# Softmax denominators in causal attention: the adds of the diagonal tiles moved from TensorE to GpSimd

## The chip, the cores and the metric

One core of a Trainium2 chip runs the whole kernel in one launch. The metric is the device time in microseconds of one execution; lower is better. The times of the kernel before are three executions.

## The reference, cut to what matters

The kernel computes one decoder layer for x of shape (2, 2048, 512): causal self-attention with 16 heads of 32 columns, cross-attention over 77 context rows, and a mixture of 8 experts, each followed by a layer norm. The change lies in the self-attention:

```python
dots = jnp.einsum('bhid,bhjd->bhij', q, k) * scale
causal_mask = jnp.triu(jnp.ones((t, t), dtype=bool), 1)
dots = jnp.where(causal_mask, -jnp.inf, dots)
attn = jax.nn.softmax(dots, axis=-1)
out = jnp.einsum('bhij,bhjd->bhid', attn, v)
```

The softmax of a query divides by the sum of its exponentials over all keys up to its own position. That sum, the denominator, is what the change computes in another way.

## The kernel before, in words

The kernel has three phases: the projections (`project`), the self-attention (`self_attention`), and everything else (`second_half`). The phases follow each other; each ends with a barrier of all engines.

**Tiles.** The self-attention goes through 8 groups (2 batches of 4 groups), each with 4 heads. In a group the 2048 queries are cut into 4 chunks of 512 (c = 0 to 3), and the keys into tiles of 128 (kt). Chunk c needs the tiles kt = 0 to 4c + 3. The last four of them lie on the diagonal: there only the queries from `off` = 0, 128, 256 or 384 on see the keys, so these tiles are 512, 384, 256 and 128 columns wide. The others are called whole. A chunk has 4, 8, 12 or 16 tiles, a group 40, and each tile has four units, one for each head: 160 units in a group.

**Steps.** All engines run the same list of steps, one step for each unit, two groups to a turn of the hardware loop (`laps`). What an engine does in a step is fixed by a lag: the function `chunk_at(s, lag)` names the chunk whose last unit lay `lag` steps ago, `tile_at(s, lag)` the tile. Each engine takes its work strictly in this order. Counted from the last unit of a chunk (step 0), and for tile j of the chunk that follows (its units are steps 4j + 1 to 4j + 4):

- step of the unit itself: TensorE makes the scores of keys by queries in `st_ps` (a ring of 3, L821 and L824), ScalarE takes the exponentials into `probs` (a ring of 5 tiles, L715).
- `VALUES` = 4: TensorE multiplies the tile with the values into `o_ps` (L841), four heads side by side, fp32.
- `SUMS` = 6: TensorE multiplies the tile with ones into `den_ps` (L859): the denominator. This is done for the diagonal tiles and for every third whole tile.
- lag 1: GpSimd adds the other whole tiles (kt % 3 is not 2) into `total` (L623). The tiles 0, 1, 3, 4, 6 and so on are taken; the first add reads tiles 0 and 1 and so comes with tile 1. Tile j is added in step 4j + 5. After the last sum of a chunk TensorE multiplies `total` with ones (L864) and closes the denominator.
- steps 5 and 7: ScalarE moves `o_ps` to `o_raw` (L721) and `den_ps` to `den` (L725).
- `RECIPS` = 9, 11, 13, 15: VectorE takes the reciprocal of `den` in four pieces (L767).
- `SCALED` = 16: GpSimd multiplies `o_raw` by `den` into `o_sb` (L629).
- step 18: VectorE makes the fp16 high part of `o_sb` (L772, a copy with a cast). Step 19: GpSimd subtracts it for the low part (L633). Step 20: SyncE stores both.

**The row maxima.** Beside this, and ahead of it, TensorE makes the same scores as queries by keys in `s_ps` (a ring of 3, L804 and L807) and VectorE reduces each to its row maxima (L746). When a chunk's maxima are complete, three small VectorE instructions make `max_parts` of them (L750, L752, L755), TensorE turns these to rows (L793), VectorE moves the rows out (L742) and SyncE copies them into `q_pair`, where the score matmuls of the chunk take them in. This side work (`AUX`) is spread over the steps by a planner (`schedule`) that weighs VectorE's costs. By its plan the rows of chunk 3 are turned in the second unit of the third diagonal tile of chunk 2, those of chunk 2 at unit 10 of chunk 1 (9 after the change), those of the next group's chunk 0 at unit 10 of chunk 3 (9 after), and those of its chunk 1 in the middle of chunk 3. Counted here from 1.

**Order.** TensorE's step is: scores, one piece of side work, values, sums, the rest of the side work. VectorE's step is: side work, reciprocals, cast. GpSimd's step is: add, multiply, subtract.

Of the kernel before, what the change touches and what calls it, by code (L numbers as in the profile page):

```python
# [6 lines left out]
ALU, ACT, AX = mybir.AluOpType, mybir.ActivationFunctionType, mybir.AxisListType  # L7
# [6 lines left out]
P = 128  # L14
# [5 lines left out]
CPB = T // CH  # L20
TT = CH // P
# [380 lines left out]
def self_attention(nc, S, x_rows, q_parts, k_parts, v_rows, o_parts):  # L402
# [17 lines left out]
    for c in range(CPB):  # L420
# [1 line left out]
    NKU, NVU, NAUX = len(KU), len(VU), len(AUX)  # L422


    POOLED = [[n for n, (k, kt) in enumerate(KU) if k == c and kt < c * TT and kt % 3 != 2]
              for c in range(CPB)]
    ADDS = [n for tiles in POOLED for n in tiles[1:]]
    NP = 5
# [1 line left out]
    PIECES = 4  # L430

    VALUES, SUMS = 4, 6
    TAKEN = VALUES + 1, SUMS + 1
    RECIPS = [SUMS + 3 + 2 * n for n in range(PIECES)]
    SCALED = RECIPS[-1] + 1
    STORED = SCALED + 4
    TAIL = STORED + 1
# [96 lines left out]
    with ExitStack() as stack:  # L534
# [31 lines left out]
        st_ready = Count(nc, stack, "st_ready", 2 * NVU)  # L566
        exp_done = Count(nc, stack, "exp_done", 2 * NVU)
        pv_done = Count(nc, stack, "pv_done", 2 * NKU)
        o_ready = Count(nc, stack, "o_ready", 2 * CPB)
        o_taken = Count(nc, stack, "o_taken", 2 * CPB)  # L570
        den_taken = Count(nc, stack, "den_taken", 2 * CPB)
        added = Count(nc, stack, "added", 2 * len(ADDS))
# [11 lines left out]
        def _(pool):  # L584
# [25 lines left out]
            def step(i, s, first, end):  # L610
                k = tile_at(s, 1, first, end)
                if k is not None and k % NKU in ADDS:
                    c, n = KU[k % NKU][0], adds_upto(k) - 1
                    starts = k % NKU == POOLED[c][1]
                    pool.wait_ge(exp_done.sem, exp_done.at(i, HG * k + HG - 1))
                    if starts:

                        pool.wait_ge(pv_done.sem, pv_done.at(i, k // NKU * NKU + LAST_TILE[c - 1]))
                        other = probs[:, (k // NKU * NKU + POOLED[c][0]) % NP]
                    else:  # L620
                        pool.wait_ge(added.sem, added.at(i, n - 1))
                        other = total[:]
                    nc.gpsimd.tensor_tensor(total[:], other, probs[:, k % NP], ALU.add).then_inc(added.sem, 1)  # L623
                c = chunk_at(s, SCALED, first, end)
                if c is not None:

                    pool.wait_ge(recips.sem, recips.at(i, c * PIECES + PIECES - 1))
                    pool.wait_ge(split_done.sem, split_done.at(i, c - 1))
                    nc.gpsimd.tensor_tensor(o_sb[:], o_raw[:], den[:], ALU.mult).then_inc(scaled.sem, 1)  # L629
                c = chunk_at(s, SCALED + 3, first, end)  # L630
                if c is not None:
                    pool.wait_ge(o_hi_done.sem, o_hi_done.at(i, c))
                    nc.gpsimd.tensor_tensor(o_out[:, c % 2, 1], o_sb[:], o_out[:, c % 2, 0],  # L633
                                            ALU.subtract).then_inc(split_done.sem, 1)
# [64 lines left out]
        def _(act):  # L699
# [4 lines left out]
            def step(i, s, first, end):  # L704
# [11 lines left out]
                                         scale=SCALE).then_inc(exp_done.sem, 1)  # L716
                c = chunk_at(s, TAKEN[0], first, end)
                if c is not None:
                    act.wait_ge(o_ready.sem, o_ready.at(i, c))
                    act.wait_ge(scaled.sem, scaled.at(i, c - 1))  # L720
                    nc.scalar.activation(o_raw[:], o_ps[:], ACT.Copy).then_inc(o_taken.sem, 1)  # L721
                c = chunk_at(s, TAKEN[1], first, end)
                if c is not None:
                    act.wait_ge(pv_done.sem, pv_done.at(i, c // CPB * NKU + LAST_TILE[c % CPB]))
                    nc.scalar.activation(den[:], den_ps[:], ACT.Copy, scale=1.0 / XS).then_inc(den_taken.sem, 1)  # L725

            laps(act, step)
# [49 lines left out]

        @block.tensor
        def _(pe):
            for count in (st_ready, pv_done, o_ready, s_ready):  # L780
                count.lead(pe)

            def aux(i, n):
# [45 lines left out]
            def values(i, k):  # L829
# [12 lines left out]
                                            start=(kt == 0), stop=final)  # L842
                if k % NKU in POOLED[c]:
                    last.then_inc(pv_done.sem, 1)
                elif final:
                    last.then_inc(o_ready.sem, 1)

            def sums(i, k):

                c, kt = KU[k % NKU]  # L850
                off, pooled = max(kt - c * TT, 0) * P, POOLED[c]
                final = k % NKU == LAST_TILE[c]
                if k % NKU in pooled:
                    return
                opens = all(n in pooled for n, (x, _) in enumerate(KU) if x == c and n < k % NKU)
                if opens:
                    pe.wait_ge(den_taken.sem, den_taken.at(i, k // NKU * CPB + c - 1))
                for h, out in enumerate(heads):
                    last = nc.tensor.matmul(den_ps[out, off:], ones[:], probs[:, k % NP, h, off:], start=opens,  # L859
                                            stop=final and not pooled)  # L860
                if final and pooled:
                    pe.wait_ge(added.sem, added.at(i, adds_upto(k) - 1))
                    for h, out in enumerate(heads):
                        last = nc.tensor.matmul(den_ps[out, :], ones[:], total[:, h], start=False, stop=True)  # L864
                last.then_inc(pv_done.sem, 1)

            def step(i, s, first, end):
                p = unit_at(s, 0, first, end)
# [8 lines left out]
                k = tile_at(s, SUMS, first, end)  # L877
                if k is not None:
                    sums(i, k)
                for n in todo[1:]:  # L880
                    aux(i, n)

# [672 lines left out]
```

## Time and profile before

| | us |
|---|---|
| three executions | 2785.82, 2792.28, 2791.89 |
| median | 2791.89 |
| the profiled execution, its own time | 2788.14 |
| its span, first to last instruction | 2786.3 |
| TensorE busy (92% of the span) | 2563.3 |
| VectorE busy (69%) | 1913.3 |
| ScalarE busy (40%) | 1102.4 |
| GpSimd busy (28%) | 782.0 |

The self-attention lies between about 325 and 1517 us. Engines in the rows: PE is TensorE (matmuls), PEld its weight loads, DVE VectorE, ACT ScalarE, POOL GpSimd, SP SyncE. A row of a timeline has the start, the duration, the engine, the line and operation, output and inputs, the shapes, and the number of instructions merged into it; in brackets stands how long the engine was idle before it and what ended that. One fp32 matmul of L841, L859 or L864 is recorded as two, so one tile with its four heads is 8 records.

### The profile page before, as it was taken

Reading aid. Unit: us, or ns where it says so; the run is one execution under the profiler, and the core shown is the slowest. Engines: PE = TensorE matmul, PEld = TensorE weight load, DVE = VectorE, ACT = ScalarE, POOL = GpSimd, SP = SyncE. Lnnn points to the kernel's source line nnn. Section 1 sums busy time; section 2 is a strip of 40 time slices with the busy share of each in tenths; the row PEclk is TensorE's granted clock in tenths of the full one; section 3 lists DMA queues with packets and bytes.
Section 4 is the critical chain, followed back from the end, with each engine's and each line's share of the span. In section 5 each row is a group of like instructions: output and inputs, shape, how many; then the busy total and the mean of one; then the engine's idle time right before and its main releaser. Section 6 shows DMA issues by size and latency. Waiting matters only on the chain. (4 is left out here: it accounts for less than half of the span.)

```text
span 2786.3 us, 44691 instructions
## 1 busy us (share of the span) xinstructions
PE 2563.3 (92%) x15124; PEld 1064.3 (38%) x15124; DVE 1913.3 (69%) x3125; ACT 1102.4 (40%) x2002; POOL 782.0 (28%) x276
## 2 busy tenths in 40 slices
PE   8999699998999899999998679999999999999998
PEld 3444223232232233332322335454544544454543
DVE  5442787877778677778882557776867676767764
ACT  4231155555555455555555223231323323232320
POOL 0000254553636344445455211111201011111100
PEclk9999799999999999999999889999999999999999
DMA  7953500302020302012001210101010101001000
GB/s 245 306 193 140 122 9 6 73 6 70 9 69 9 69 6 55 23 34 74 5 12 56 86 43 1 58 1 59 1 43 16 43 16 43 16 1 58 1 16 16
DMA packets 115902, 146.74 MB, mean 53 GB/s; under 512 B 9086, under 2 KB 87678, under 8 KB 114653
## 3 DMA queue, kind: packets, MB, share of 16 engines
q1 hardware_dynamic: 115677, 143.77, 16.9%
q8 instruction: 138, 2.26, 0.3%
q14 instruction: 87, 0.71, 0.1%
HBM read 91.57 MB, written 51.91 MB: 51 GB/s over the span
## 5 line engine op out<-in xcount | busy, mean ns | idle before, releaser
L715 ACT ACTIVATE probs<-st_ps 128x512 f32<-128x512 f32 (+3 forms) x1280 | 628.2, 533 | 590.5 <-PE st_ps L821 294.6
L746 DVE TENSOR_REDUCE seg_max<-s_ps 128x1 f32<-128x512 f32 (+3 forms) x1280 | 699.8, 599 | 230.3 <-PE s_ps L804 136.9
L804 PE MATMUL s_ps<-k_pair,q_pair 96*128 96x512 f16 (+3 forms) x1280 | 438.7, 364 | 70.0 <-DVE seg_max L746 56.4
L821 PE MATMUL st_ps<-q_pair,k_pair 98*128 98x512 f16 (+3 forms) x1280 | 434.6, 360 | 26.6 <-issue 19.5
L623 POOL TENSOR_TENSOR total<-total,probs 128x2048 f32<-128x2048 f32 x88 | 398.2, 4525 | 62.1 <-ACT probs L715 59.6
L841 PE MATMUL o_ps<-probs,v_sb 128*32 128x512 f32 (+3 forms) x2560 | 321.4, 572 | 0.7 <-issue 0.7
L1381 PE MATMUL fps<-x2T,w_p_hi 128*128 128x512 f16 x1024 | 317.2, 379 | 0.0
L1381 PE MATMUL fps<-w_p_hi,hT 128*128 128x512 f16 x1024 | 306.0, 381 | 0.0
L821 PEld LDWEIGHTS st_ps<-q_pair,k_pair 98*128 98x128 f16 x1280 | 117.5, 98 | 374.4 <-ACT probs L715 287.4
L804 PEld LDWEIGHTS s_ps<-k_pair,q_pair 96*128 96x128 f16 x1280 | 125.6, 99 | 276.9 <-DVE seg_max L746 191.3
L1343 DVE SCALAR_TENSOR_TENSOR x<-fps,gates_un,x 128x512 f32<-128x512 f32 x256 | 184.0, 746 | 36.0 <-PE fps L1381 33.4
L623 POOL TENSOR_TENSOR total<-probs 128x2048 f32<-128x2048 f32 x24 | 108.8, 4533 | 354.7 <-ACT probs L715 354.7
L1168 ACT ACTIVATE hidden<-fps,keep_b_sb 128x512 f32<-128x512 f32 x128 | 86.5, 687 | 304.1 <-PE fps L1381 303.8
L1381 PE MATMUL fps<-w_p_lo,hT 128*128 128x512 f16 x512 | 194.7, 380 | 0.0
L1381 PE MATMUL fps<-x2T,w_p_lo 128*128 128x512 f16 x512 | 194.0, 379 | 0.0
L1085 POOL TENSOR_TENSOR rstd<-rstd,keep_power 128x4 f32<-128x4 f32 x24 | 26.2, 1090 | 552.0 <-DVE rstd L1206 552.0
L1100 POOL TENSOR_TENSOR soft<-soft,ssum 128x1232 f32<-128x1232 f32 x32 | 72.9, 2288 | 384.4 <-DVE ssum L1236 384.4
L1332 DVE TENSOR_SCALAR hT<-hidden 128x512 f16<-128x512 f32 x128 | 86.0, 672 | 108.1 <-ACT hidden L1168 107.5
L859 PE MATMUL den_ps<-probs,ones 128*32 128x512 f32 (+3 forms) x1472 | 156.0, 494 | 0.0
L1381 PEld LDWEIGHTS fps<-x2T,w_p_hi 128*128 128x128 f16 x1024 | 100.2, 98 | 128.8 <-issue 5.9
L1381 PEld LDWEIGHTS fps<-w_p_hi,hT 128*128 128x128 f16 x1024 | 98.1, 98 | 131.0 <-issue 20.8
L767 DVE RECIPROCAL den<-den 128x128 f32<-128x128 f32 x128 | 116.5, 927 | 44.5 <-ACT den L725 44.5
(162 smaller groups left out, 3553.7 us busy)
## 6 DMA issues: line engine op xcount, KB each, us to landing
k_pair<-k_parts SPq DMA_DIRECT2D x96, 128.0 KB, 5.0
q_pair<-q_parts SPq DMA_DIRECT2D x96, 128.0 KB, 5.6
x_raw<-xT_in SPq DMA_DIRECT2D x8, 1024.0 KB, 6.5
q_parts<-qk_out SPq DMA_DIRECT2D x32, 256.0 KB, 3.6
k_parts<-qk_out SPq DMA_DIRECT2D x32, 256.0 KB, 4.0
piece_raw<-w_in SPq DMA_DIRECT2D x8, 1024.0 KB, 8.7
v_rows<-v_out SPq DMA_DIRECT2D x32, 256.0 KB, 2.1
w_parts<-piece_cut SPq DMA_DIRECT2D x8, 1024.0 KB, 5.6
```

What stands on the lines that cost most here:

```text
L623: nc.gpsimd.tensor_tensor(total[:], other, probs[:, k % NP], ALU.add).then_inc(added.sem, 1)
L715: nc.scalar.activation(probs[:, k % NP, h, off:], st_ps[:, p % (2 * NVU) % RING, off:], ACT.Exp, scale=SCALE).then_inc(exp_done.sem, 1)
L746: nc.vector.reduce_max(seg_max[:, h, j, s:s + 1], s_ps[:, slot, 0:width], AX.X).then_inc(s_read.sem, 1)
L767: nc.vector.reciprocal(piece, piece).then_inc(recips.sem, 1)
L804: last = nc.tensor.matmul(s_ps[:, slot, 0:width], q_pair[a][0:NR, h, q0:q0 + P], k_pair[a][0:NR, h, s * CH:s * CH + width], start=True, st ...
L821: last = nc.tensor.matmul(st_ps[:, slot, off:], k_pair[a][:, h, kt * P:(kt + 1) * P], q_pair[a][:, h, c * CH + off:(c + 1) * CH], start=Tr ...
L841: last = nc.tensor.matmul(o_ps[out, off:], v_sb[a][:, kt, out], probs[:, k % NP, h, off:], start=(kt == 0), stop=final)
L859: last = nc.tensor.matmul(den_ps[out, off:], ones[:], probs[:, k % NP, h, off:], start=opens, stop=final and not pooled)
L1168: nc.scalar.activation(hidden[:, n % 2], fps[:, (u * NUNIT + f) % FB], ACT.Gelu, bias=W["b1_sb"][:, n:n + 1], scale=UN).then_inc(gelu_done ...
L1332: nc.vector.tensor_scalar(hT[:, 0, e % 2, j], hidden[:, n % 2], XS, None, ALU.mult).then_inc(h_hi.sem, 1)
L1343: nc.vector.scalar_tensor_tensor(x2[q][:, j], bank, gates_un[q][:, j, e:e + 1], x2[q][:, j], ALU.mult, ALU.add).then_inc(added.sem, 1)
L1381: last = nc.tensor.matmul(bank, lhs(a, t), rhs(b, t), start=(n == 0), stop=(n == len(steps) - 1))
```

## The change

GpSimd's list of tiles takes in the diagonal tiles as well. Its first add of chunk 0 is 384 columns wide and followed by a copy of the 128 columns that only tile 0 has. TensorE's sums are left for every third whole tile only; `total` is multiplied with ones in a step of its own, `TOTALS` = 8, for all four chunks (before: chunks 1 to 3, in step 6). The steps that hang on it follow two later: `den` is moved in step 9, the reciprocals are in steps 11, 13, 15 and 17, the multiply in step 18, the cast in step 20, the subtraction in step 21, the store in step 22. The first add of a chunk waits for the totals of the chunk before. SyncE's loads for the group after next wait for `pv_done` of a group's last tile, which now comes with its values.

```diff
-    POOLED = [[n for n, (k, kt) in enumerate(KU) if k == c and kt < c * TT and kt % 3 != 2]
+    POOLED = [[n for n, (k, kt) in enumerate(KU) if k == c and (kt >= c * TT or kt % 3 != 2)]
               for c in range(CPB)]
...
     VALUES, SUMS = 4, 6
-    TAKEN = VALUES + 1, SUMS + 1
-    RECIPS = [SUMS + 3 + 2 * n for n in range(PIECES)]
+    TOTALS = 8
+    TAKEN = VALUES + 1, TOTALS + 1
+    RECIPS = [TOTALS + 3 + 2 * n for n in range(PIECES)]
     SCALED = RECIPS[-1] + 1
...
                     pool.wait_ge(exp_done.sem, exp_done.at(i, HG * k + HG - 1))
+                    off = max(KU[k % NKU][1] - c * TT, 0) * P
                     if starts:
-                        pool.wait_ge(pv_done.sem, pv_done.at(i, k // NKU * NKU + LAST_TILE[c - 1]))
+                        pool.wait_ge(den_ready.sem, den_ready.at(i, k // NKU * CPB + c - 1))
                         other = probs[:, (k // NKU * NKU + POOLED[c][0]) % NP]
                     else:
                         pool.wait_ge(added.sem, added.at(i, n - 1))
                         other = total[:]
-                    nc.gpsimd.tensor_tensor(total[:], other, probs[:, k % NP], ALU.add).then_inc(added.sem, 1)
+                    last = nc.gpsimd.tensor_tensor(total[:, :, off:], other[:, :, off:], probs[:, k % NP, :, off:],
+                                                   ALU.add)
+                    if starts and off:
+                        last = nc.gpsimd.tensor_copy(total[:, :, 0:off], other[:, :, 0:off])
+                    last.then_inc(added.sem, 1)
...
-                    act.wait_ge(o_ready.sem, o_ready.at(i, c))
+                    act.wait_ge(pv_done.sem, pv_done.at(i, c // CPB * NKU + LAST_TILE[c % CPB]))
                     act.wait_ge(scaled.sem, scaled.at(i, c - 1))
...
-                    act.wait_ge(pv_done.sem, pv_done.at(i, c // CPB * NKU + LAST_TILE[c % CPB]))
+                    act.wait_ge(den_ready.sem, den_ready.at(i, c))
...
             def sums(i, k):
                 c, kt = KU[k % NKU]
-                off, pooled = max(kt - c * TT, 0) * P, POOLED[c]
-                final = k % NKU == LAST_TILE[c]
-                if k % NKU in pooled:
+                if k % NKU in POOLED[c]:
                     return
...
                 for h, out in enumerate(heads):
-                    last = nc.tensor.matmul(den_ps[out, off:], ones[:], probs[:, k % NP, h, off:], start=opens,
-                                            stop=final and not pooled)
-                if final and pooled:
-                    pe.wait_ge(added.sem, added.at(i, adds_upto(k) - 1))
-                    for h, out in enumerate(heads):
-                        last = nc.tensor.matmul(den_ps[out, :], ones[:], total[:, h], start=False, stop=True)
+                    last = nc.tensor.matmul(den_ps[out, :], ones[:], probs[:, k % NP, h], start=opens, stop=False)
                 last.then_inc(pv_done.sem, 1)
+
+            def totals(i, c):
+                opens = all(n in POOLED[c % CPB] for n, (x, _) in enumerate(KU) if x == c % CPB)
+                if opens:
+                    pe.wait_ge(den_taken.sem, den_taken.at(i, c - 1))
+                pe.wait_ge(added.sem, added.at(i, adds_upto(c // CPB * NKU + LAST_TILE[c % CPB]) - 1))
+                for h, out in enumerate(heads):
+                    last = nc.tensor.matmul(den_ps[out, :], ones[:], total[:, h], start=opens, stop=True)
+                last.then_inc(den_ready.sem, 1)
...
                 k = tile_at(s, SUMS, first, end)
                 if k is not None:
                     sums(i, k)
+                c = chunk_at(s, TOTALS, first, end)
+                if c is not None:
+                    totals(i, c)
```

## Rows read from the trace of the kernel before

**Rows 1.** The page, part 1: busy time and share of the span

```profile
PE 2563.3 (92%) x15124; PEld 1064.3 (38%) x15124; DVE 1913.3 (69%) x3125; ACT 1102.4 (40%) x2002; POOL 782.0 (28%) x276
```

**Rows 2.** Stretches: busy us of each engine, granted clock share (PEclk), DMA share, GB/s

```profile
340.00:1517.00 1177.00, 1086.01 (x7734) 350.29 (x7734) 900.26 (x1483) 645.29 (x1327) 582.65 (x176) 0.96 0.13 32
```

**Rows 3.** Groups by shape, 440 to 1520 us: busy us, mean ns of one record

```profile
L859 PE MATMUL den_ps<-probs,ones 128*32 128x512 f32 x648 | 86.7, 604 | 0.0
...
L859 PE MATMUL den_ps<-probs,ones 128*32 128x384 f32 x232 | 24.7, 498 | 0.0
...
L864 PE MATMUL den_ps<-total,ones 128*32 128x512 f32 x176 | 22.9, 592 | 0.0
...
L859 PE MATMUL den_ps<-probs,ones 128*32 128x256 f32 x232 | 18.5, 391 | 0.0
...
L859 PE MATMUL den_ps<-probs,ones 128*32 128x128 f32 x232 | 12.8, 294 | 0.0
```

**Rows 4.** TensorE's timeline: one denominator sum and the matmul behind it

```profile
622.82 1.06 PE L859 MATMUL den_ps<-probs,ones 128*32 128x512 f32 x8
...
623.82 0.28 PE L821 MATMUL st_ps<-q_pair,k_pair 98*128 98x256 f16 x1
```

**Rows 5.** Single lines: duration ns min/median/max, first and last start us

```profile
L772 DVE CAST o_out<-o_sb x32: 415/3682/4746, 358.9 to 1515.5; 128x512 f16<-128x512 f32 x32
...
L752 DVE TENSOR_SCALAR max_parts<-row_max x32: 174/175/1448, 294.5 to 1461.0; 128x16 f16<-128x16 f32 x32
...
L755 DVE SCALAR_TENSOR_TENSOR max_parts<-row_max,max_parts x32: 174/174/176, 295.5 to 1461.3; 128x16 f16<-128x16 f32 x32
```

**Rows 6.** Timelines of POOL, DVE, ACT and PE, start of chunk 2 of a group

```profile
692.12 1.27 POOL L629 TENSOR_TENSOR o_sb<-o_raw,den 128x512 f32<-128x512 f32 x1 [1.71 <-DVE den L767]
693.36 4.52 POOL L623 TENSOR_TENSOR total<-total,probs 128x2048 f32<-128x2048 f32 x1
...
694.94 3.22 DVE L772 CAST o_out<-o_sb 128x512 f16<-128x512 f32 x1
...
689.74 2.07 ACT L715 ACTIVATE probs<-st_ps 128x512 f32<-128x512 f32 x4 [1.20 <-PE st_ps L821]
...
694.55 1.09 ACT L715 ACTIVATE probs<-st_ps 128x512 f32<-128x512 f32 x2 [1.10 <-PE st_ps L821]
...
698.69 0.39 PE L804 MATMUL s_ps<-k_pair,q_pair 96*128 96x512 f16 x1 [1.98 <-DVE seg_max L746]
```

**Rows 7.** Stretches behind two stalls, and the longer stall in TensorE's timeline

```profile
699.90:703.70 3.80, 3.59 (x12) 0.57 (x12) 2.78 (x5) 1.22 (x3) 3.80 (x1) 0.55 0.19 69
...
649.80:655.80 6.00, 5.99 (x28) 1.35 (x29) 2.19 (x5) 2.87 (x6) 1.94 (x1) 0.50 1.00 226
...
649.81 0.61 PE L821 MATMUL st_ps<-q_pair,k_pair 98*128 98x512 f16 x1 [5.99 <-issue]
```

**Rows 8.** Timelines, start of chunk 3 of the last group, and its end

```profile
1472.01 4.54 POOL L623 TENSOR_TENSOR total<-probs 128x2048 f32<-128x2048 f32 x1 [12.13 <-ACT probs L715]
...
1477.73 4.55 POOL L623 TENSOR_TENSOR total<-total,probs 128x2048 f32<-128x2048 f32 x1
...
1477.82 4.75 DVE L772 CAST o_out<-o_sb 128x512 f16<-128x512 f32 x1 [2.96 <-POOL o_sb L629]
...
1510.15 0.60 ACT L725 ACTIVATE den<-den_ps 128x512 f32<-128x512 f32 x1 [0.48 <-PE den_ps L864]
```

**Rows 9.** Timelines of ACT, DVE and PE, diagonal tiles of chunk 2

```profile
555.02 2.20 ACT L715 ACTIVATE probs<-st_ps 128x512 f32<-128x512 f32 x4 [1.15 <-PE st_ps L824]
...
559.98 0.17 DVE L752 TENSOR_SCALAR max_parts<-row_max 128x16 f16<-128x16 f32 x1
...
560.68 0.33 PE L793 MATMUL s_ps<-ident,max_parts 128*8 128x128 f16 x3
```

**Rows 10.** TensorE's timeline in chunk 0: its unit 7, and unit 5 of chunk 1

```profile
486.50 0.34 PE L821 MATMUL st_ps<-q_pair,k_pair 98*128 98x384 f16 x1
...
495.95 0.39 PE L821 MATMUL st_ps<-q_pair,k_pair 98*128 98x512 f16 x1
```

More of the change, by code:

```diff
@@ L568, in self_attention @@
         pv_done = Count(nc, stack, "pv_done", 2 * NKU)
-        o_ready = Count(nc, stack, "o_ready", 2 * CPB)
+        den_ready = Count(nc, stack, "den_ready", 2 * CPB)
         o_taken = Count(nc, stack, "o_taken", 2 * CPB)
@@ L779, in _ @@
         def _(pe):
-            for count in (st_ready, pv_done, o_ready, s_ready):
+            for count in (st_ready, pv_done, den_ready, s_ready):
                 count.lead(pe)
@@ L844, in values @@
                     last.then_inc(pv_done.sem, 1)
-                elif final:
-                    last.then_inc(o_ready.sem, 1)
             def sums(i, k):
                 c, kt = KU[k % NKU]
-                off, pooled = max(kt - c * TT, 0) * P, POOLED[c]
-                final = k % NKU == LAST_TILE[c]
-                if k % NKU in pooled:
+                if k % NKU in POOLED[c]:
                     return
-                opens = all(n in pooled for n, (x, _) in enumerate(KU) if x == c and n < k % NKU)
+                opens = all(n in POOLED[c] for n, (x, _) in enumerate(KU) if x == c and n < k % NKU)
                 if opens:
```

## The prediction

> **What bounds the kernel now.** I read the busy shares first: TensorE works 92% of the span [rows 1]. The row for the attention alone says 1086 of 1177 us for TensorE, 900 for VectorE and 583 for GpSimd [rows 2]. So TensorE sets the pace, a matmul taken away there is worth its slot, and GpSimd has room on average. Then I asked where TensorE's missing 91 us go. The timeline around a chunk's start answers it [rows 6]: VectorE's cast L772 takes 3.22 us, while its shortest takes 0.415 us and its median 3.68 us [rows 5]. It lies over a GpSimd add of 4.52 us and ends just after it. TensorE runs out of free `s_ps` slots and stands still for 1.98 us. This happens once in each of chunks 1, 2 and 3 (24 times; I found stalls of 1.7 to 2.7 us). So the copying cast cannot run while GpSimd adds. The order of GpSimd's queue is therefore part of TensorE's path, and this is what the change moves.
>
> After such a stall TensorE's clock falls. Behind the 1.98 us stall the granted clock is 0.55 for 3.8 us, practically 1.2 GHz in place of 2.4, which costs about 1.8 us. Behind the stall of 5.99 us at the loop's turn it is 0.50 for 6.0 us, which costs 3.0 us [rows 7].
>
> **The change, part by part.** The sum is made against the profiled execution's own time, 2788.1 us, which is 0.13% under the median of the three runs.
>
> *Sums removed on TensorE.* The groups by shape give 1.07, 0.85, 0.64 and 0.44 us busy for a tile of 512, 384, 256 and 128 columns (86.7 us for 648 records, 8 to a tile; 24.7, 18.5 and 12.8 us for 232) [rows 3]. The next matmul starts 1.00 us after the start of a 512 sum that is 1.06 long [rows 4], so a slot is 0.07 shorter or so: 1.00 + 0.78 + 0.57 + 0.36 = 2.7 us for each of 32 chunks, 86.7 us. Chunk 0 gets a total that it did not have, 8 x 1.0 us. The totals of the other chunks only move. Net: **-78 us**. I take all of it, as TensorE is the pace there. If exponentials (ScalarE) were late in the short tiles, perhaps 10 us of it would be lost.
>
> *GpSimd's load.* An operation on 512 elements takes 1.27 us, one on 2048 takes 4.52 [rows 6], so by a line through both 1024 take 2.4 and 1536 take 3.4. The four diagonal adds are 11.6 us, those of chunk 0 with its copy about 7.7 (the copy of 512 elements is not in the trace; between 0.2 and 1.27 us, I take 0.6, half of the nearest row, as it reads one operand). That is 42.5 us a group, 340 in all, and raises GpSimd to 923 of 1177 us. It does not become the bound on average, and its total is there in time: the diagonal adds end some 4 to 5 us after a chunk's last exponential, and TensorE asks for them 8 steps later, 6 us or more.
>
> *The chunk start, chunks 1 to 3.* Before, GpSimd's queue was: multiply (step 16), add of tile 3 (17), while the cast stood in step 18. Now it is: add of tile 3 (17), multiply (18), add of tile 4 (21), with the cast in step 20. The multiply waits behind one add, and the cast behind the multiply and then behind the next add. In the chunk shown: the exponentials of tile 3 end at 689.74 + 2.07 = 691.8, so the add of tile 3 runs from 691.9 to 696.4 and the multiply to 697.7. The exponentials of tile 4 ended at 695.6, so its add follows at once, to 702.2. The cast ends at 702.6, one reduction frees a slot, and TensorE goes on at 703.2 instead of 698.7 [rows 6]. It stands two steps further on by then. Between the exponentials at 689.74 and 694.55 lie six steps, so two are 1.6 us, and the loss is 4.5 - 1.6 = 2.9 us more than before. Does the add really get in ahead of the waiting cast? At the start of the last group's chunk 3 VectorE had waited 2.96 us for the multiply, the add began 0.1 us before the cast, and the cast took 4.75 us, the longest of all [rows 8]. So yes. 23 starts (that last one has no reductions left to hold up): **+67 us**. The lower end is a gain (the third rival), the upper 3.2 us each, 74. The stalls grow to about 5 us, between the two of rows 7; I take 2.4 us for the slow clock behind each in place of 1.8: **+14 us**.
>
> The Trainium skill has the rule in "SBUF — State Buffer", section "SBUF: two separate sides": VectorE and GpSimd share a port pair that is an exclusive lock for the whole instruction, taken by whichever starts first. By that rule the trace agrees with its 4.75 us cast, and the sum stays the same.
>
> *The rows of chunk 3.* `max_parts` are made while chunk 2's diagonal tiles are exponentiated. Before, no GpSimd add ran then. Now the add of tile 8 starts when its exponentials end, at 557.2, and runs to 561.8; L752 would start at 559.98, inside it [rows 9]. L752 can be held up: its median is 0.175 us, its longest 1.448 [rows 5]. At 561.8 the add of tile 9 is ready too and takes 3.4 us, to 565.3. If it gets in first, as in rows 8, L752 and L755 end at about 565.7 instead of 560.35. TensorE needs them at 560.68 and has nothing to pass the time with, since the turn L793 stands in its queue: 5.0 us x 8 = **+40 us**, and 2.4 us of slow clock x 8 = **+19 us**. If VectorE gets in first with both, it is 1.8 us a group. L755 itself was never slowed (176 ns at most [rows 5]).
>
> The same section of the Trainium skill says that VectorE operations with two SBUF inputs, which L755 is, need the pair as well; then the add of tile 9 would come between L752 and L755 if not before both, and the whole 5 us would be paid either way. No row here shows it.
>
> *Chunk 0.* The cast of chunk 3 comes in step 20, when chunk 1 of the next group has begun, and ScalarE's `o_raw` in step 21 waits for the same multiply. GpSimd's chain from the total on is 3.4 + 0.6 + 2.4 + 1.3 + 1.3, with gaps some 9.5 us. TensorE has from unit 7 to unit 5 of chunk 1 9.45 us [rows 10], less two units and a values step (2.0) and three sums (2.35), plus four more units, values and total that it can still do (3.6): 8.7 us. So it waits about 1 us, in 5 of the 7 boundaries (**+5 us**; at the other two it stands at the loop's turn anyway). Bounds: 0 and 3 us each. The group loads on SyncE start some 2 us earlier; nothing waited for them but the loop's turn, whose 6 us I leave as they are.
>
> *The end.* Chunk 3 of the last group has no side work and GpSimd is its pace. From its first add at 1472.01 to ScalarE's `den` at 1510.15 it took 38.1 us [rows 8]. Now the chain is 7 adds of 4.52, the multiply and subtraction (2.5), the cast (0.4), the diagonal adds (11.6) and the total (1.0): 47.2 us, so 9 us more, and the 2.7 us of sums counted above are not won: **+12 us**.
>
> Sum: -78 + 67 + 14 + 40 + 19 + 5 + 12 = +79, so **2867 us**.
>
> **The rivals.** *A, the forecast*, 2867 us; its own range is 2845 to 2892 from the ends named above. Chance 0.45.
>
> *B, VectorE gets in at the end of the add of tile 8.* Then the rows cost 1.8 us and about 1 us of clock a group, 22 in place of 59: 2830 us. For it: L752 has been waiting for 2 us by then, while the cast of rows 8 had only just been released. Chance 0.22.
>
> *C, more of the small instructions are caught.* Chunk 2's `max_parts` fall half a microsecond before the first add of chunk 1 starts; if that add gets them, up to 4.5 us x 8 come on top, or the slow clock lasts longer than I took: about 2900 us. Chance 0.15.
>
> *D, faster.* The cast gets in between the multiply and the add of tile 4. The point that decides is that instant, 24 times. The cast would end at 698.1 where VectorE reaches it at 696.5, no TensorE stall remains, and the old ones go too (24 x 2.1 us and 24 x 1.8 us of clock): -78 - 51 - 43 + 14 + 5 + 12 = -141, 2647 us. A mixture of both outcomes would lie just under the old time. Against it stands the 4.75 us cast. Chance 0.13.
>
> *E, the terms cancel.* The stalls grow by 1 us only, because the reductions left in the ring carry TensorE further, and the rows as in B: -78 + 23 + 22 + 17 = -16, up to +10 with the clock. Chance 0.05.
>
> **How the numbers follow.** A and C end over, B too. The range goes from half way between B and E, 2805, to C's upper part, 2905; it leaves D, E and the far end out. A measurement here tells 0.3%, 8 us, from no change. Faster: D and part of E, 0.14. The same: 0.05. Slower: 0.81.
>
> **What would show it.** Right: the median of L772 at 5 to 7 us or, where the wait for the multiply is counted apart, casts near 4.7 behind idle time; TensorE stalls of 4 to 5 us at the starts of chunks 1 to 3; L752 or L755 at 2 to 5 us once a group, and as much idle before L793; GpSimd busy near 1120 us of the span; TensorE's L859 down to 448 records, L864 up to 256. Wrong: casts of 0.4 us behind the multiply, or TensorE stalls as short as before. Waits of L864 for the adds would be a further rival that I give no weight.

## The result and the profile after

The changed kernel takes 2874.06 us (median of 4 runs, 2871.89 to 2876.44) against 2790.48 us for the kernel before in the same comparison: a ratio of 1.0302, with an interval of 1.0284 to 1.032. It is slower, as forecast. The profiled execution took 2871.89 us against 2788.14 before, 83.8 us more. In the changed kernel the lines of the code stand 6 further down for VectorE, ScalarE and TensorE's score steps (the cast L772 is now L778, L752 and L755 are L758 and L761, the turn L793 is L799, the reductions L746 are L752), and 2 further down for GpSimd's add (L625); its multiply L629 is now L635, its copy L628. TensorE's values are L847, its sums L861 and its totals L871. ScalarE's exponentials are L721, `o_raw` is L727 and `den` L731.

The page of the kernel after, its busy times, the granted clock and GpSimd over 40 slices, and the group of the cast (columns as in [rows 1]):

```profile
PE 2512.6 (88%) x14164; PEld 1063.0 (37%) x14164; DVE 1960.2 (68%) x3125; ACT 1094.8 (38%) x2002; POOL 1119.7 (39%) x404
...
POOL 0001377776677767776778321020112111111100
PEclk9999889898898989898999779999999999999999
...
L778 DVE CAST o_out<-o_sb 128x512 f16<-128x512 f32 x32 | 115.2, 3600 | 67.1 <-POOL o_sb L635 67.1
```

GpSimd is busy for 1119.7 us, the 1120 of the prediction, and the 32 casts wait 67.1 us in all for the multiply L635 and then run for 3.6 us on average. The 24 at the starts of chunks 1 to 3 take 4.6 to 4.75 us each, the 8 others 0.43 us.

The attention's stretch of the kernel after, which is 84 us longer than in [rows 2] (same columns), and the stretch around the stall at a start of chunk 2:

```profile
340.00:1601.00 1261.00, 1034.48 (x6776) 347.55 (x6772) 942.00 (x1478) 636.01 (x1325) 913.00 (x300) 0.90 0.12 29
...
719.50:726.50 7.00, 7.00 (x22) 1.91 (x23) 4.57 (x9) 2.17 (x4) 0.56 (x1) 0.54 0.12 40
```

TensorE's work in the attention fell from 1086.0 to 1034.5 us, so 51.5 us were won. But its idle time rose from 91.0 to 226.5 us, by 135.5. The difference is the 84 us that the kernel lost. The waits of TensorE over the whole execution say who ended that idle time (us in all, how often, the longest), first in the kernel before, then after:

```profile
PE s_ps L804 <- DVE seg_max L746: 56.4, 49, 2.7
...
PE s_ps L793 <- DVE max_parts L755: 13.2, 9, 2.8
```

```profile
PE s_ps L810 <- DVE seg_max L752: 137.5, 55, 5.8
PE s_ps L799 <- DVE max_parts L761: 39.1, 17, 3.1
PE o_ps L847 <- ACT o_raw L727: 12.8, 5, 3.0
```

The third had no counterpart before. Taken one by one, the 23 stalls at the starts of chunks 1 to 3 rose from 50.8 to 130.5 us. All but one (5.09 us) are now 5.6 to 5.8 us long, where they were 1.7 to 2.7. The timeline of the kernel after around the same start of chunk 2 as in [rows 6] shows why (start, duration, engine, line, operation, and in brackets the idle time before it and its releaser):

```profile
708.32 4.54 POOL L625 TENSOR_TENSOR total<-total,probs 128x2048 f32<-128x2048 f32 x1 [1.18 <-ACT probs L721]
...
712.83 1.27 POOL L635 TENSOR_TENSOR o_sb<-o_raw,den 128x512 f32<-128x512 f32 x1
...
714.05 4.50 POOL L625 TENSOR_TENSOR total<-total,probs 128x2048 f32<-128x2048 f32 x1
...
714.13 4.70 DVE L778 CAST o_out<-o_sb 128x512 f16<-128x512 f32 x1 [2.06 <-POOL o_sb L635]
...
719.49 0.61 PE L810 MATMUL s_ps<-k_pair,q_pair 96*128 96x512 f16 x1 [5.76 <-DVE seg_max L752]
```

The multiply stands behind the add of tile 3. When it ends, the add of tile 4 is already queued and starts at once, 0.08 us ahead of the cast that the end of the multiply released. The cast then takes 4.70 us, where its shortest takes 0.43, and ends 0.28 us behind the add. VectorE's reductions stand behind it, TensorE gets no free slot of `s_ps`, and stands still for 5.76 us.

The diagonal of chunk 2 in the kernel after, which answers to [rows 9]:

```profile
572.58 4.51 POOL L625 TENSOR_TENSOR total<-total,probs 128x2048 f32<-128x2048 f32 x1
...
577.17 3.46 POOL L625 TENSOR_TENSOR total<-total,probs 128x1536 f32<-128x1536 f32 x1
...
573.60 3.53 DVE L758 TENSOR_SCALAR max_parts<-row_max 128x16 f16<-128x16 f32 x1
577.16 0.18 DVE L761 SCALAR_TENSOR_TENSOR max_parts<-row_max,max_parts 128x16 f16<-128x16 f32 x1
577.39 0.28 PE L799 MATMUL s_ps<-ident,max_parts 128*8 128x128 f16 x2 [3.03 <-DVE max_parts L761]
```

L758 can do nothing until the add of tile 8 ends (572.58 plus 4.51 is 577.09) and is done at 577.13. L761 starts at 577.16, 0.01 us ahead of the add of tile 9. That is one stall of 3.0 to 3.1 us in each of the 8 groups.

The last group's chunk 3 in the kernel after, from GpSimd's first add to ScalarE's `den` (same columns):

```profile
1544.70 4.54 POOL L625 TENSOR_TENSOR total<-probs 128x2048 f32<-128x2048 f32 x1 [2.77 <-PE den_ps L871]
...
1591.94 1.93 PE L871 MATMUL den_ps<-total,ones 128*32 128x512 f32 x8 [10.62 <-POOL total L625]
1593.94 0.60 ACT L731 ACTIVATE den<-den_ps 128x512 f32<-128x512 f32 x1 [11.95 <-PE den_ps L871]
```

It takes 49.2 us, against 38.1 in [rows 8]. TensorE's wait of 10.62 us for the last add is part of it.

### The profile page after: what moved, and what is told of

It reads as the page before. It is cut to its first block and busy times, and to the rows that moved or that the text cites. A ratio compares the mean times of both kernels' runs of the same rounds, so it can differ in the third digit from the quotient of the medians.

```text
span 2870.1 us, 43117 instructions
## 1 busy us (share of the span) xinstructions
PE 2512.6 (88%) x14164; PEld 1063.0 (37%) x14164; DVE 1960.2 (68%) x3125; ACT 1094.8 (38%) x2002; POOL 1119.7 (39%) x404
## 5 line engine op out<-in xcount | busy, mean ns | idle before, releaser
L721 ACT ACTIVATE probs<-st_ps 128x512 f32<-128x512 f32 (+3 forms) x1280 | 619.9, 536 | 654.3 <-PE st_ps L827 336.3
L752 DVE TENSOR_REDUCE seg_max<-s_ps 128x1 f32<-128x512 f32 (+3 forms) x1280 | 697.8, 598 | 177.1 <-PE s_ps L810 91.0
L625 POOL TENSOR_TENSOR total<-total,probs 128x2048 f32<-128x2048 f32 (+3 forms) x200 | 704.8, 3524 | 190.2 <-ACT probs L721 180.3
L810 PE MATMUL s_ps<-k_pair,q_pair 96*128 96x512 f16 (+3 forms) x1280 | 448.8, 375 | 153.7 <-DVE seg_max L752 137.5
L847 PE MATMUL o_ps<-probs,v_sb 128*32 128x512 f32 (+3 forms) x2560 | 328.3, 587 | 12.9 <-ACT o_raw L727 12.8
L625 POOL TENSOR_TENSOR total<-probs 128x2048 f32<-128x2048 f32 (+1 forms) x32 | 136.3, 4259 | 176.2 <-PE den_ps L871 138.1
L778 DVE CAST o_out<-o_sb 128x512 f16<-128x512 f32 x32 | 115.2, 3600 | 67.1 <-POOL o_sb L635 67.1
```

Source lines behind the costliest of these rows:

```text
L625: last = nc.gpsimd.tensor_tensor(total[:, :, off:], other[:, :, off:], probs[:, k % NP, :, off:], ALU.add)
L721: nc.scalar.activation(probs[:, k % NP, h, off:], st_ps[:, p % (2 * NVU) % RING, off:], ACT.Exp, scale=SCALE).then_inc(exp_done.sem, 1)
L752: nc.vector.reduce_max(seg_max[:, h, j, s:s + 1], s_ps[:, slot, 0:width], AX.X).then_inc(s_read.sem, 1)
L778: nc.vector.tensor_copy(o_out[:, c % 2, 0], o_sb[:]).then_inc(o_hi_done.sem, 1)
L810: last = nc.tensor.matmul(s_ps[:, slot, 0:width], q_pair[a][0:NR, h, q0:q0 + P], k_pair[a][0:NR, h, s * CH:s * CH + width], start=True, st ...
L847: last = nc.tensor.matmul(o_ps[out, off:], v_sb[a][:, kt, out], probs[:, k % NP, h, off:], start=(kt == 0), stop=final)
```

## The experiments

The theory (Q): GpSimd's own work costs nothing. What costs is that VectorE's copying instructions (the cast, the first of `max_parts`) can't run under a GpSimd add, and that the longer queue puts the multiply and the cast among the adds. One rival (L) says that 340 us more of GpSimd's work slow VectorE or the `probs` ring as such. Another (W) says that the cast only comes late, because the multiply waits behind an add, and VectorE's queue stands behind it. The results, each against the kernel before in the same comparison:

| run | median us | kernel before | ratio, interval |
|---|---|---|---|
| e1 change, cast on ScalarE | 2736.6 | 2789.15 | 0.9812, 0.9784 to 0.984 |
| e2 before, cast on ScalarE | 2723.7 | 2789.15 | 0.9767, 0.9737 to 0.9798 |
| e3 change, cast 4 steps later | 2791.11 | 2789.15 | 1.0005, 0.999 to 1.002 |
| e4 change without tile 4 | 2769.92 | 2789.15 | 0.9938, 0.992 to 0.9957 |
| e5 before, 11 of 16 sums left out | 2736.03 | 2790.49 | 0.9807, 0.9792 to 0.9821 |
| e6 change without tile 8 of chunk 2 | 2880.48 | 2790.49 | 1.0326, 1.0309 to 1.0342 |
| e7 change, two `o_raw` | 2900.32 | 2790.49 | 1.0392, 1.0375 to 1.0409 |
| e8 e1, two `o_raw`, high half on ScalarE | 2714.48 | 2790.49 | 0.9729, 0.9713 to 0.9745 |
| e10 e8, low half elsewhere too | 2666.16 | 2788.28 | 0.9564, 0.9549 to 0.9579 |
| e11 before, with e10's edits | 2702.57 | 2788.28 | 0.97, 0.9683 to 0.9717 |

**e1 and e2: the cast goes to ScalarE.** In both kernels the cast leaves VectorE. In e2 the steps are two lower, as TOTALS is not there.

```
-    STORED = SCALED + 4
+    STORED = SCALED + 8          (e2: + 6)
 ScalarE:
+                c = chunk_at(s, SCALED + 6, first, end)      (e2: + 4)
+                if c is not None:
+                    act.wait_ge(scaled.sem, scaled.at(i, c))
+                    act.wait_ge(o_stored[c % 2], stored_at(CPB * i + c // 2))
+                    nc.scalar.activation(o_out[:, c % 2, 0], o_sb[:], ACT.Copy).then_inc(o_hi_done.sem, 1)
 VectorE:
-                    nc.vector.tensor_copy(o_out[:, c % 2, 0], o_sb[:]).then_inc(o_hi_done.sem, 1)
```

> The changed kernel with the fp16 cast of o_sb moved from VectorE (step 20) to ScalarE (step 24, the subtraction follows in step 25). Theory Q (GpSimd's queue and the pair that VectorE's cast needs): the TensorE stalls of 5.6 to 5.8 us at the starts of chunks 1 to 3 vanish, 23 x 5.7 = 131 us, and most of the slow clock behind them (24 times 6.8 us at half speed, up to 80 us): 2660 to 2700 us. Rival L (GpSimd's 338 us of added work are the cost, whoever casts): within 10 us of the changed kernel, 2860 to 2880 us. Rival W (the wait for the late multiply is the cost, not the add that runs over the cast): ScalarE now waits in its place and TensorE's stalls come from the exponentials, about 2 us each: some 2790 us.

> The kernel before with the same cast on ScalarE (step 20, subtraction in step 21). Theory Q: its 24 stalls of 1.7 to 2.7 us (51 us) and the 1.7 us of slow clock behind each (41 us) vanish: about 2700 us. Rival L says nothing of it; if the stalls were only where TensorE loses slack that it needs anyway, under 20 us are won: 2770 us or more.

The changed kernel falls by some 137 us, to 2736.6, and the stalls at the chunk starts are gone. L falls as the main cause, since GpSimd does all the work of the change here. The kernel before gains 65 us by the same edit, so these stalls cost it as well; 89 were expected. And e1 misses its expectation by 37 us and stays 13 us behind e2. The waits of TensorE in e1 say where that is:

```profile
PE s_ps L801 <- DVE max_parts L768: 55.4, 18, 4.0
PE o_ps L849 <- ACT o_raw L728: 17.6, 7, 3.0
...
PE den_ps L873 <- POOL total L625: 15.3, 9, 10.6
```

and in e2:

```profile
PE s_ps L795 <- DVE max_parts L762: 23.6, 10, 4.1
```

So with the long stalls gone, the small instructions of `max_parts` and the late `o_raw` (0 us in e2) take 49 us more in e1 than in e2, and the waits for the adds (0 us in e2) another 15. Those are 65 of the 78 us of removed sums. The mean granted clock is lower too, 0.951 in e1 against 0.963 in e2; what that alone costs was not measured.

**e3: the cast stays on VectorE, four steps later.**

```
-    STORED = SCALED + 4
+    STORED = SCALED + 8
-                c = chunk_at(s, SCALED + 2, first, end)
+                c = chunk_at(s, SCALED + 6, first, end)      (the cast, on VectorE)
```

> The changed kernel with the cast still on VectorE, but four steps later (24 in place of 20; subtraction in 25). Theory Q: VectorE meets the add of tile 4 near its end instead of before its start, waits about 2.5 us in place of 6.5, and TensorE's stalls shrink from 5.7 to 1 or 2 us: 23 x 4 = 92 us and half of the slow clock behind them, 40 us: 2720 to 2760 us. Rival L: unchanged, 2870 us.

The cast in e3, as a single line (shortest, median and longest in ns, first and last start):

```profile
L778 DVE CAST o_out<-o_sb x32: 419/2480/4748, 364.2 to 1512.2; 128x512 f16<-128x512 f32 x32
```

83 us come back. The wait for the multiply is gone, but the cast still falls under some add: its median is 2.48 us, and the 23 stalls take 51.0 us, about what they took in the kernel before. I had expected at least 31 us more. A shift in steps changes how much of an add the cast meets, not that it meets one. The edit takes away W's wait and shortens the time under the add at once, so the 83 us can't be given to W alone. But W can't be all of it, as e1 has the same slack and is 55 us faster.

**e4: tile 4 of chunks 1 to 3 stays with TensorE.** No add is then queued right behind the multiply.

```
-    POOLED = [[n for n, (k, kt) in enumerate(KU) if k == c and (kt >= c * TT or kt % 3 != 2)]
+    POOLED = [[n for n, (k, kt) in enumerate(KU) if k == c and (kt >= c * TT or kt % 3 != 2) and not (c and kt == 4)]
```

> The changed kernel with tile 4 of chunks 1 to 3 summed by TensorE (24 sums of 1.0 us more) and not added by GpSimd, so that no add is queued behind the multiply when the cast is due. It keeps the wait for the multiply (1.2 to 2.0 us) and takes away the add over the cast. Theory Q: casts of 0.4 us, TensorE stalls under 1 us at those places: 2870 + 24 - 120 - 70 = about 2700 us. Rival W (the wait counts): stalls of 2 us stay, 2790 us. Rival L: GpSimd loses 108 us of work of 338, so a third of the loss, 2845 us.

The cast in e4, as a single line:

```profile
L778 DVE CAST o_out<-o_sb x32: 426/427/429, 362.5 to 1494.8; 128x512 f16<-128x512 f32 x32
```

All 32 casts now take 0.43 us, and the casts wait as long for the multiply as in the changed kernel (67.2 us in all against 67.1): one tile apart, 4.70 us have become 0.43. This is the cleanest proof that the add behind the multiply is what holds the cast. But 22 stalls of 1.3 to 1.9 us (33 us) stay. That is W's part, the wait for the multiply behind the add of tile 3. The time, 2769.9, lies nearer to W's 2790 than to Q's 2700. So of the 5.7 us of a stall some 1.5 are W's, and some 4 are the add's.

**e5: the kernel before with 11 of its 16 diagonal sums left out.** TensorE's gain alone, with nothing given to GpSimd: the denominators lack those tiles.

```
-                if k % NKU in POOLED[c]:
+                if k % NKU in POOLED[c] or left_out(k):
+            def left_out(k):
+                c, kt = KU[k % NKU]
+                return kt >= c * TT and kt < c * TT + 3 and kt > 0
```

> The kernel before with 11 of the 16 sums of diagonal tiles of a group left out on TensorE and given to nobody: the denominators miss those tiles. It measures the change's first term alone, with nothing added on GpSimd. By the slots, 3 x (1.00 + 0.78 + 0.57) + (0.78 + 0.57) = 8.4 us a group, 67 us in all. Theory Q: all of it is won, 2720 to 2730 us. Rival N (TensorE is not the pace in the short tiles, the exponentials are): half of it or less, 2750 us or more.

Of the 67 us expected 54.5 came. TensorE's busy time in the attention fell from 1084.9 to 1025.4 us, by 59.5, and the stalls stayed at 51 us. The 7.5 us of busy time that are missing go with the clock: its mean granted share over the span is 0.957 in the kernel before and 0.951 here. At two levels that is an estimated 240 and 268 us at the lower one, so up to 14 us lost. Another 3.5 us are TensorE's waits for exponentials (6.4 us before, 9.9 here), a small part of what rival N had forecast. The price by slot was about right, and the clock takes roughly a tenth of the gain.

**e6: tile 8 of chunk 2 stays with TensorE.** The add which held the first of `max_parts` is gone, and the add of tile 9 (1536 elements) is the next.

```
-    POOLED = [[n for n, (k, kt) in enumerate(KU) if k == c and (kt >= c * TT or kt % 3 != 2)]
+    POOLED = [[n for n, (k, kt) in enumerate(KU) if k == c and (kt >= c * TT or kt % 3 != 2) and not (c == 2 and kt == 8)]
```

> The changed kernel with the first diagonal tile of chunk 2 (tile 8) summed by TensorE, so that no long add runs while the row maxima of chunk 3 are made. Costs 8 sums, 8 us. Theory Q: the 3.0 us wait of the turn of rows, 8 times, goes, and with it some 12 us of slow clock: 2874 - 24 - 12 + 8 = about 2845 us. It also shows whether the third small instruction (two SBUF inputs) is held by the next add, of 1536 elements, which starts just then: if it is, waits of 3 us stay and the time is 2880 us.

The timeline of e6 on VectorE and GpSimd at the rows of chunk 3:

```profile
572.90 0.17 DVE L758 TENSOR_SCALAR max_parts<-row_max 128x16 f16<-128x16 f32 x1
573.08 3.42 POOL L625 TENSOR_TENSOR total<-total,probs 128x1536 f32<-128x1536 f32 x1 [1.31 <-ACT probs L721]
573.11 3.41 DVE L761 SCALAR_TENSOR_TENSOR max_parts<-row_max,max_parts 128x16 f16<-128x16 f32 x1
```

Nothing is won: the first instruction runs in 0.17 us, the add starts, and now the second, which starts 0.03 us behind it, is held for 3.41 us (3.33 to 3.42 in each of the 8 groups). It reads two SBUF operands of 128x16. This is the sentence of the Trainium skill that the prediction could not show by a row ("SBUF — State Buffer", section "SBUF: two separate sides": VectorE operations with two SBUF inputs need the shared pair too, against a GpSimd operation that reads SBUF, as this add does). By that rule, e6 agrees with 3.41 us against 0.18.

**e7: two buffers for `o_raw`.** ScalarE no longer waits for the multiply before it empties `o_ps`.

```
-        o_raw = sb("o_raw", [P, CH], F32)
+        o_raw = sb("o_raw", [P, 2, CH], F32)
-                    act.wait_ge(scaled.sem, scaled.at(i, c - 1))
-                    nc.scalar.activation(o_raw[:], o_ps[:], ACT.Copy).then_inc(o_taken.sem, 1)
+                    act.wait_ge(scaled.sem, scaled.at(i, c - 2))
+                    nc.scalar.activation(o_raw[:, c % 2], o_ps[:], ACT.Copy).then_inc(o_taken.sem, 1)
...
+                    act.wait_ge(scaled.sem, scaled.at(i, c - 1))       (ahead of den)
```

> The changed kernel with two buffers for o_raw, so that ScalarE's step 21 does not wait for the multiply of the chunk before. Theory Q: TensorE's wait of 2.4 to 3.0 us in chunk 1's second tile (5 times, 12.8 us) goes with 8 us of slow clock, if nothing comes in its place: 2855 us. VectorE's cast waits 3.0 us for the same multiply, so a stall of 1 us may take its place: 2862 us.

A miss in sign. The 12.8 us of waits for `o_raw` are gone, and the kernel is 26 us slower. The waits of TensorE in e7, and under them the place in its timeline:

```profile
PE s_ps L800 <- DVE max_parts L762: 69.0, 22, 6.2
```

```profile
509.85 4.49 POOL L625 TENSOR_TENSOR total<-probs 128x2048 f32<-128x2048 f32 x1
...
510.73 3.65 DVE L759 TENSOR_SCALAR max_parts<-row_max 128x16 f16<-128x16 f32 x1
```

Chunk 2's `max_parts` now fall under the first add of chunk 1, in 5 groups: stalls of 6.0 us where there were none. This is the mechanism of rival C. In these 5 groups L758 (here L759) starts 2.53 us behind the end of chunk 0's multiply in both kernels. What moved is the add: it starts 1.65 us behind that end here, and 3.3 to 4.3 us behind it in the changed kernel, where the profile has it wait for chunk 0's total on TensorE (1.98 us in one such place). TensorE had stood still there for `o_raw`. So the wait for `o_raw` was what held the add back; that is read from the two timelines and was not tested apart.

**e8: e1, two `o_raw`, and the high half of `max_parts` on ScalarE.** L758 leaves VectorE. The two-input instruction stays.

```
+            def high(i, n):
+                if AUX[(n + 1) % NAUX][0] == "rows":
+                    k = n // NAUX * CPB + AUX[n % NAUX][1]
+                    act.wait_ge(steps.sem, steps.at(i, 2 * k))
+                    nc.scalar.activation(max_parts[:, 0], row_max[:], ACT.Copy,
+                                         scale=-1.0 / QK).then_inc(steps.sem, 1)
 VectorE:
-                    nc.vector.tensor_scalar(max_parts[:, 0], row_max[:], -1.0 / QK, None,
-                                            ALU.mult).then_inc(steps.sem, 1)
```

> The changed kernel with three edits: the cast on ScalarE (as in the first run), the high half of max_parts on ScalarE too (it was a VectorE instruction that waits for GpSimd's adds), and two buffers for o_raw. Theory Q: against the first of these runs (2736.6 us) the waits for max_parts (49.6 us on TensorE) fall to about 5, the waits for o_raw (17.6 us) go, and some 30 to 50 us of slow clock: 2736 - 45 - 17 - 40 = about 2635 us; what stays is the end of the last group, 10.6 us. If the third small instruction is now the one that is held, or TensorE finds the next wait (reductions, exponentials), 2690 us.

The second instruction of `max_parts` in e8, as a single line:

```profile
L777 DVE SCALAR_TENSOR_TENSOR max_parts<-row_max,max_parts x32: 174/758/4148, 295.6 to 1369.3; 128x16 f16<-128x16 f32 x32
```

It now has a median of 758 ns and a longest of 4.1 us: its partner no longer runs just ahead of it on VectorE. TensorE still waits 44.7 us for it. The time misses the 2635 us expected by 79, and even the 2690 named for this case by 24.

**e10 and e11: no VectorE instruction that needs the pair.** ScalarE also writes the two terms of the low half side by side, and VectorE adds them with a reduction, which reads one operand. The same edits on the kernel before make e11 (with one `o_raw`).

```
+        pair = sb("max_pair", [P, HG, TT, 2], F32)
 ScalarE, behind the high half:
+                    nc.scalar.activation(pair[:, :, :, 0], row_max[:], ACT.Copy, scale=-1.0 / QK)
+                    act.wait_ge(halves.sem, halves.at(i, k))
+                    nc.scalar.activation(pair[:, :, :, 1], max_parts[:, 0], ACT.Copy,
+                                         scale=-1.0).then_inc(steps.sem, 1)
 VectorE:
-                    nc.vector.scalar_tensor_tensor(max_parts[:, 1], row_max[:], -1.0 / QK, max_parts[:, 0], ALU.mult,
-                                                   ALU.subtract).then_inc(max_ready.sem, 1)
+                        nc.vector.tensor_reduce(max_parts[:, 1], pair[:], AX.X, ALU.add).then_inc(max_ready.sem, 1)
```

> The kernel of e8 (the change, cast and high half on ScalarE, two buffers for o_raw) in which the low half of max_parts is made without an instruction of two SBUF inputs: ScalarE puts the scaled maxima and minus the high half beside each other, VectorE adds the pairs with a reduction. Theory Q (every VectorE instruction that needs the pair is gone, reductions are never held): TensorE's 16 waits for max_parts fall from 40 us to about 10 and the slow clock behind them by some 30 us at half speed: 2714 - 30 - 15 = about 2670 us. If the reduction of two SBUF columns is held too: 2715 to 2720 us.

> The same edits on the kernel before (cast, high half on ScalarE, low half by a reduction; one o_raw). Against the second run (2723.7 us) the waits for max_parts, 19.7 us, fall to about 8, with 5 to 10 us of slow clock: 2705 us. Theory Q: without shared-pair waits the change is worth its sums, 78 us, less the end of the last group (10 to 13 us) and what the clock takes back: this run should be 35 to 60 us slower than e10. Rival L (GpSimd's added work costs by itself): e10 is not faster than this one.

The reduction in e10 as a single line, the attention's stretch (columns as in [rows 2]), and TensorE's waits for the adds:

```profile
L785 DVE TENSOR_REDUCE max_parts<-max_pair x32: 185/186/188, 294.9 to 1319.8; 128x16 f16<-128x32 f32 x32
```

```profile
340.00:1389.00 1049.00, 974.88 (x6773) 331.12 (x6773) 786.11 (x1418) 656.11 (x1444) 911.38 (x300) 0.98 0.14 35
```

```profile
PE den_ps L889 <- POOL total L627: 23.1, 17, 10.6
```

and the attention's stretch in e11:

```profile
340.00:1428.00 1088.00, 1045.14 (x7718) 347.88 (x7716) 794.19 (x1417) 663.94 (x1447) 581.88 (x176) 0.99 0.14 34
```

All 32 reductions take 185 to 188 ns, whatever GpSimd does, and TensorE's waits for `max_parts` fall from 44.7 to 6.8 us. Both met their expectations: 2666.2 and 2702.6 us. So with nothing for GpSimd's adds to hold up, the change wins 36.4 us instead of losing 83.6, with GpSimd busy for 911 of 1049 us. (e10 has a second `o_raw` besides, which e11 lacks; TensorE never waits for `o_raw` in e11.) e10 is 4.4% faster than the kernel before and the best of all. Of the 78 us of sums, about half still doesn't arrive. TensorE's busy time in the attention is 70 us shorter in e10 than in e11, but its idle time is 31 us longer, 74 against 43. 23.1 us of it are waits for the adds, 10.6 of them at the very end, and e11 has none. So L, which had fallen as the cause of the loss, names a cost of that size, and the prediction had given such waits no weight but for the end.

## Why the prediction was right, and where it was off

The mechanism is the one forecast, A with B's outcome at one of its places. The time is 7 us above 2867, measured, and 5 by the profiled execution (2871.9). That it came so near is partly luck: terms that were off by up to 16 us cancelled. Of the signs named, the casts near 4.7 us, L758 at 3.5 us once a group, GpSimd's 1120 us and both record counts came as forecast; the stalls were longer than the 4 to 5 us named.

*Sums, -78.* Counts and shapes are as forecast. By shape, the kernel after has

```profile
L861 PE MATMUL den_ps<-probs,ones 128*32 128x512 f32 x448 | 59.7, 605 | 0.0
...
L871 PE MATMUL den_ps<-total,ones 128*32 128x512 f32 x256 | 39.6, 695 | 10.6 <-POOL total L625 10.6
```

e5 supports the price by slot: 59.5 us of busy time for 67 forecast, with a lower mean clock.

*Chunk starts, +67.* The step was right and a size was off: the stalls grew by 3.5 us each, 80 in all. From the start of the add behind the multiply to TensorE's next matmul it took 5.44 us (714.05 to 719.49), and I had 5.5 (697.7 to 703.2). What failed is "It stands two steps further on by then". TensorE ran dry 0.3 us before that add began (719.49 less 5.76 is 713.73), where my sum had it 0.6 us behind (698.7 less 1.98, plus 1.6, is 698.3). D, the gain, fell: the add gets in first, and what it would have been worth is what e4 and e1 show.

*Rows of chunk 3, +40.* This step failed in its arbitration and in a start time. "If it gets in first, as in rows 8" did not happen. The waiting L758 got its turn at the add's end, before the queued add of tile 9, as rival B had it. Nor did that add come between L758 and L761, as the sentence behind it expected: L761 was 0.01 us ahead in the group shown and took 0.18 us. In e6 it did come between. But B's 1.8 us were too short: it had the add of tile 8 start when its exponentials end. In the kernel before, an add of tile 7 was still running then, in a line that I had not read:

```profile
549.71 9.13 POOL L623 TENSOR_TENSOR total<-total,probs 128x2048 f32<-128x2048 f32 x2 [2.39 <-ACT probs L715]
```

It ends at 558.84, so the add of tile 8 ends 1.6 us later than I had it. That gives 3.4, and 3.0 to 3.1 were measured, 24 us in all. The term was 16 us too high.

*Slow clock, +14 and +19.* TensorE's busy time fell by 51.5 where the slots give 78. The 27 us between them are a remainder, near to the 33 forecast, and I put them down to the clock; e5 says that some 8 of them come with the removal of the sums. The mean granted clock fell from 0.957 to 0.933, an estimated 240 and 385 us at the lower level. At half pace these 145 us more would cost 72, well over 27. Part of them lies in the stalls, where no matmul is slowed; how much the rest cost no run shows.

*Chunk 0, +5.* 12.8 us, in 5 boundaries as forecast, but 2.4 to 3.0 us each. GpSimd's chain at such a boundary of the kernel after:

```profile
493.48 3.46 POOL L625 TENSOR_TENSOR total<-probs 128x1536 f32<-128x1536 f32 x1 [3.66 <-PE den_ps L871]
496.88 0.61 POOL L628 COPY total<-probs 128x512 f32<-128x512 f32 x1
497.57 2.35 POOL L625 TENSOR_TENSOR total<-total,probs 128x1024 f32<-128x1024 f32 x1
500.00 1.26 POOL L625 TENSOR_TENSOR total<-total,probs 128x512 f32<-128x512 f32 x1
501.23 1.26 POOL L635 TENSOR_TENSOR o_sb<-o_raw,den 128x512 f32<-128x512 f32 x1
```

Each duration is as forecast, the guess of 0.6 for the copy too, and the chain is 9.0 us long. ScalarE's move of `o_raw`, which my sum left out, adds 0.7, until TensorE goes on at 503.23. The larger part was lost on TensorE's side: it stopped at 500.78, 7.3 us behind the chain's start, where I had it work for 8.7.

*The end, +12.* 11.1 us longer, where I had 9, and 2.7 us of sums not won: 14 against 12.

The sum came out right since the starts and chunk 0 were 21 us too low, and the rows 16 and the clock some 6 too high. Of the rivals, C was not there in the changed kernel. It is real, though: e7 has it, in stalls of 30 us in all. The waits for the adds, which the prediction gave no weight, were 10.6 us at the very end and nowhere else.

## What to carry to other kernels

Before work goes to GpSimd, list the VectorE instructions that can't run under a GpSimd one (here the copying f32 to f16 cast and the small scaling on one SBUF operand, and the instruction on two SBUF operands), and look at what follows each in GpSimd's queue, not only at GpSimd's load: at 911 of 1049 us it cost TensorE 23 us of waits once they were gone, and the change still won 36. If such an instruction lies on the path, give it to ScalarE or to a form that isn't held, such as the reduction here, and only then move the work. Where a wait is taken away, look again at which work now starts sooner, and at what falls under it (e7).

## What the runs showed of the hardware

- In this kernel a VectorE instruction that was released by the very end of a GpSimd one lost to the add queued behind it (cast 4.6 to 4.75 us at 24 chunk starts, against 0.43 us without such an add in e4). One that had been standing through an add got in at its end, ahead of the next queued add (L758, 3.5 to 3.6 us in 8 groups, with L761 at 0.18 behind it).
- The two-input instruction was not held in the kernel before (176 ns at most) and hardly in the changed one (516 ns at most). In e6, where an add started 0.03 us ahead of it, it was held for 3.41 us; in e8 for up to 4.15 us. A row that shows an instruction at its short time is no proof that it can't be held.
- Behind a stall of 5.76 us the granted clock was 0.54 over 7.0 us, which loses about 3.2 us; behind 1.98 us it was 0.55 over 3.8 us [rows 7]. With the sums left out and the stalls as before (e5), the mean granted clock fell from 0.957 to 0.951.
- A VectorE reduction of 128x32 took 185 to 188 ns in all 32 cases, with GpSimd busy for 911 of the attention's 1049 us (e10).
